# One third of the gate and up rows computed with the two matrices side by side, its last 21 rows without shared products

## The chip, the cores and the metric

The kernel runs on one core of a Trainium2 chip. The metric is the device time of one execution in microseconds. The core's engines run side by side and meet only at semaphores: TensorE (PE; its weight loads are listed apart as PEld), VectorE (DVE), ScalarE (ACT), GpSimd (POOL) and SyncE (SP, which issues most DMAs here).

## The reference, cut to what matters

A token has 1024 numbers, which are 8 components of 128. A small matrix per batch entry is applied first, then a feed-forward net whose linear maps are octonion products with ternary weights:

```python
y = einsum('bct,bcd->bdt', x, cond_weights[itok])            # (32, 64, 1024): 2048 tokens
gate = oct_ternary_linear(y, w_gate)                         # 8 components of 341 rows
up   = oct_ternary_linear(y, w_up)
h    = silu(gate) * up
out  = x + oct_ternary_linear(h, w_down)
# oct_ternary_linear: M = einsum('jik,jod->koid', S_OCT, Wq);  out = einsum('...id,koid->...ko', xp, M)
```

S_OCT holds a sign for every pair of components, so each output component k is a sum over the 8 input components i of a signed 341 x 128 matrix times y_i. Wq is -1, 0 or 1 times one scale for each of w_gate, w_up and w_down.

## The kernel before, in words

The 2048 tokens are cut into 8 tiles T of 256. Every operand of a large product is split into two float16 parts, "hi" and "lo", so each product is two matmuls (the loop over e). The 341 rows of a component are three windows w: 128, 128 and 85, the last padded with zeros to 128. A chunk c is one window of a pair of components (K, K+4), with both matrices m (0 gate, 1 up): 12 chunks a tile, c = 4w + K.

Sign relations between the components let the products be shared. A table (`gate_table`, `up_table`, built once in tile 0) holds sums and differences of weight blocks, and `y_op` holds the 8 components and 6 sums of them (14 operands). Of a chunk, PE makes (all through `group`, L1013 to L1018, whose every matmul is 128 x 128 weights times 256 tokens):

- `shared_pair` (even chunks only): 2 matrices x 2 terms x 2 parts = 8 matmuls into `bank_q`;
- `shared`: 8 matmuls into `bank_pr(s)`, s = c % 2;
- `own`: 2 matrices x 2 halves h x 4 terms x 2 parts = 32 matmuls into `bank_r(s, 0)` for gate and `bank_r(s, 1)` for up.

A bank is 512 float32 on 128 partitions. Chunks alternate between two sets of three banks. ACT (`chunk`, L640 to L654) copies the shared product out (`q_sb`, L646), applies SiLU to the gate bank in place (L652), and in `split_h` of the chunk before copies h to float16 (`h_op`, hi part, L613) and to float32 (`h_f`, L618). DVE (`chunk`, from L847) makes p = shared product +- q (L723), subtracts for the lo part of the h before (`h_lo`, L825), adds p to the gate bank and then to the up bank (L843, or two half-width L723 operations for K = 1), and multiplies SiLU(gate) by up (L870). These queues are in order. `own` of a chunk waits until `h_lo` and `h_f` of the chunk two before are done, since that frees the gate bank; `shared` waits for the p two before.

After the chunks comes `down`: for each window 64 products with `h_op` (`down_c`, 128 columns) and 32 with `z_op` (`down_u`, 256 columns) over both halves of the tile, 288 matmuls in all (L1108). `z_op` is made from `h_f` in six rounds k, two a window: POOL adds pairs and then the results (`round_of_z`, L531; k = 5 on DVE), ACT rounds to float16 (`z_hi`, L632), DVE makes the lo part (`z_lo`, L830). `Z_LO_AFTER` says after which chunk z_hi and z_lo of a round are queued: {6: 0, 7: 1, 10: 2, 11: 3}. POOL also turns the sums of the tile before back to outputs (`back`, L443).

The next tile's operands are made inside this one: `y_round(T + 1, r)` (L1003) after chunks 1, 2, 4 and 5 (`Y_AFTER`), each followed on ACT by `copy_y` (L588, L591), which the next `y_round` waits for since all use one bank; `row_norms` (L1010) after chunk 7; and on DVE `scales_of_tile` (L782 to L809) after chunk 8. Tile 7 has none of these. In tile 0, DVE also makes the ternary weights (`ternary`, L747 and L749) and the tables (`build_table`) of window 1 after chunks 0 and 2 and of window 2 after chunks 4 and 6, and PE and ACT mix the down weights (`mix`, L981, `mix_out`, L667) at chunks 6 to 11; ACT makes `down_c` (L705) after chunks 8 to 11.

SP's DMAs load x, the residual and the small matrices and store the outputs; their order is not touched.

## Time and profile before

| | |
|---|---|
| median of 3 runs | 723.91 us (722.75 to 724.21) |
| the profiled execution | 724.41 us, of which span 722.6 us |
| PE, PEld busy | 95%, 86% |
| DVE, ACT, POOL busy | 75%, 46%, 49% |
| granted TensorE clock, mean | 0.987 of full |

A share of busy time is a mean over the whole span. The chain of waits goes back from the last instruction to whatever released it, so an engine's share of that chain says how much of the time it alone set. In a timeline the start of an instruction and the start of the next one on the same engine lie less than one duration apart when the two overlap; "idle before" names the engine and line that ended a wait.

### The profile page before, as it was taken

What the parts mean: (1) busy time and instruction counts of PE and PEld (TensorE: products, weight loads), DVE (VectorE), ACT (ScalarE), POOL (GpSimd) and SP (SyncE); (2) the same over time, 40 slices, a digit from 0 to 9 for tenths busy, and PEclk for the clock granted to TensorE, in tenths of its full rate; (3) what the DMA queues carried; (4) which work ended last, traced back from release to release, by engine and by line L of the source; (5) the groups of instructions that cost most, each with busy time, mean ns of one, the idle gap of its engine ahead of it and who ended that gap; (6) DMA issues with size and microseconds to landing.
All of it is one profiled execution on the core that took longest, in us unless ns stands there. A gap on an engine that the chain in (4) does not pass through costs nothing.

```text
span 722.6 us, 17130 instructions
## 1 busy us (share of the span) xinstructions
PE 687.3 (95%) x7046; PEld 625.0 (86%) x7046; DVE 538.6 (75%) x867; ACT 332.3 (46%) x530; POOL 352.5 (49%) x409
## 2 busy tenths in 40 slices
PE   3679998999999999999999999999999999999995
PEld 3468887999999989999899999999899998988895
DVE  1898956767876688676877678766877678777877
ACT  5543485155444546255452555344452554434531
POOL 0200557435736466344856356364753357464553
PEclk9799999999999999999999999999999999999999
DMA  8100003021002110031001110031000300021001
GB/s 327 59 2 1 1 2 122 30 89 64 1 2 88 33 61 2 2 118 63 1 2 52 66 63 2 2 117 62 4 1 11 108 2 1 2 88 31 1 2 59
DMA packets 10576, 31.51 MB, mean 44 GB/s; under 512 B 3330, under 2 KB 3330, under 8 KB 10370
## 3 DMA queue, kind: packets, MB, share of 16 engines
q1 hardware_dynamic: 9906, 28.81, 11.2%
q10 hardware_dynamic: 592, 1.61, 0.7%
q8 instruction: 56, 0.92, 0.5%
q14 instruction: 22, 0.18, 0.1%
HBM read 22.02 MB, written 8.39 MB: 42 GB/s over the span
## 4 chain that ended last, share of the span: by engine, by line
PE 85%; DVE 7%; ACT 3%; issue 2%; POOL 1%; DMA 1%; ACTq 0%; DVEq 0%; POOLq 0%
PE ps L1016 58%; PE ps L1108 21%; PE ps L1003 4%; DMA cond_bd<-in_L_cond_weights_dram 1%; DVE pu_sb L723 1%; ACT down_c L705 1%; POOL z_f L531 1%; PE ps L1010 1%; DVE o_sb L443 1%; ACT z_op L632 1%; DVE ps L843 1%; POOL h_pairs L531 1%; DVE z_op L830 0%; ACT ps L652 0%; DVE gate_table L723 0%
## 5 line engine op out<-in xcount | busy, mean ns | idle before, releaser
L1016 PE MATMUL ps<-y_op,gate_table 128*128 128x256 f16 x2112 | 273.0, 275 | 5.7 <-DVE y_op L816 4.2
L1016 PE MATMUL ps<-y_op,up_table 128*128 128x256 f16 x2112 | 270.7, 273 | 0.2 <-DVE up_table L768 0.2
L1016 PEld LDWEIGHTS ps<-y_op,gate_table 128*128 128x128 f16 x2112 | 207.6, 99 | 30.6 <-DVE y_op L816 4.3
L1016 PEld LDWEIGHTS ps<-y_op,up_table 128*128 128x128 f16 x2112 | 207.1, 98 | 25.1 <-DVE up_table L768 0.7
L531 POOL TENSOR_TENSOR h_pairs<-h_f 128x256 f32<-128x256 f32 (+1 forms) x128 | 121.1, 975 | 151.8 <-ACT h_f L618 94.1
L531 POOL TENSOR_TENSOR z_f<-h_pairs 128x512 f32<-128x512 f32 x80 | 102.7, 1305 | 102.6 <-DVE z_op L830 100.8
L652 ACT ACTIVATE ps<-ps,small 128x512 f32<-128x512 f32 x96 | 63.6, 662 | 175.5 <-DVE ps L843 125.4
L443 POOL TENSOR_TENSOR o_sb<-o_sb,wd_sb 128x256 f32<-128x256 f32 (+1 forms) x150 | 88.3, 626 | 92.7 <-DVE wd_sb L891 91.5
L1108 PE MATMUL ps<-down_c,h_op 128*128 128x128 f16 x1536 | 93.1, 220 | 3.0 <-ACT down_c L705 3.0
L723 DVE TENSOR_TENSOR pu_sb<-ps,q_sb 128x512 f32<-128x512 f32 x96 | 65.8, 686 | 38.7 <-ACT q_sb L646 26.0
L1108 PEld LDWEIGHTS ps<-down_c,h_op 128*128 128x128 f16 x1536 | 89.8, 98 | 4.0 <-ACT down_c L705 3.1
L1108 PE MATMUL ps<-down_u,z_op 128*128 128x256 f16 x768 | 90.8, 274 | 1.5 <-DVE z_op L830 1.5
L830 DVE TENSOR_TENSOR z_op<-z_f,z_op 128x1024 f16<-128x1024 f32 x40 | 49.8, 1246 | 44.7 <-ACT z_op L632 44.7
L825 DVE TENSOR_TENSOR h_op<-ps,h_op 128x512 f16<-128x512 f32 x96 | 65.8, 685 | 23.0 <-ACT h_f L618 23.0
L1108 PEld LDWEIGHTS ps<-down_u,z_op 128*128 128x128 f16 x768 | 73.9, 98 | 9.8 <-DVE z_op L830 1.6
L870 DVE SCALAR_TENSOR_TENSOR ps<-pu_sb,small,ps 128x512 f32<-128x512 f32 x96 | 72.4, 755 | 11.5 <-ACT ps L652 1.6
L613 ACT ACTIVATE h_op<-ps 128x512 f16<-128x512 f32 x96 | 57.5, 599 | 35.3 <-DVE ps L870 33.7
L843 DVE TENSOR_TENSOR pu_sb<-ps,pu_sb 128x512 f32<-128x512 f32 x72 | 49.4, 686 | 31.2 <-PE ps L1016 31.0
L632 ACT ACTIVATE z_op<-z_f 128x1024 f16<-128x1024 f32 x40 | 42.1, 1053 | 36.9 <-POOL z_f L531 36.9
L618 ACT ACTIVATE h_f<-ps 128x512 f32<-128x512 f32 x96 | 57.7, 601 | 0.0
L843 DVE TENSOR_TENSOR ps<-ps,pu_sb 128x512 f32<-128x512 f32 x72 | 49.8, 691 | 4.2 <-PE ps L1016 3.2
L1003 PE MATMUL ps<-cond_bd,x_in 128*128 128x128 f32 x256 | 35.3, 285 | 13.3 <-DMA cond_bd<-in_L_cond_weights_dram 11.1
(75 smaller groups left out, 480.7 us busy)
## 6 DMA issues: line engine op xcount, KB each, us to landing
x_in<-in_x_dram SPq DMA_DIRECT2D x8, 1024.0 KB, 5.3
o_sb<-in_x_dram SPq DMA_DIRECT2D x16, 512.0 KB, 3.6
out_dram<-o_sb SPq DMA_DIRECT2D x15, 512.0 KB, 2.7
h_op<-in_L_ffn_w_gate_dram ACTq DMA_DIRECT2D x3, 512.0 KB, 6.8
h_op<-in_L_ffn_w_up_dram SPq DMA_DIRECT2D x3, 512.0 KB, 7.4
z_op<-in_L_ffn_w_down_dram SPq DMA_DIRECT2D x1, 1536.0 KB, 11.4
out_dram<-o_sb SPq DMA_DIRECT2D x2, 256.0 KB, 2.1
cond_bd<-in_L_cond_weights_dram SPq DMA_DIRECT2D x30, 16.0 KB, 3.0
```

What stands on the lines that cost most here:

```text
L443: last = eng.tensor_tensor(dst, dst, wd_sb[:, s, k1, r0, h, :], ALU.add if sign > 0 else ALU.subtract)
L531: return pool.tensor_tensor(dst, a, b, ALU.add if sign > 0 else ALU.subtract)
L613: act.activation(h_op[:, c, :, 0, :], bank_r(s, 0), ACT.Copy).then_inc(h_hi_ready, 1)
L618: act.activation(h_f[:, c], bank_r(s, 0), ACT.Copy).then_inc(h_copied, 1)
L652: act.activation(bank_r(s, 0), bank_r(s, 0), ACT.Silu, scale=gate_scale(T)).then_inc(silu_ready, 1)
L723: return dve.tensor_tensor(dst, a, b, ALU.add if sign > 0 else ALU.subtract)
L825: dve.tensor_tensor(h_op[:, c, :, 1, :], bank_r(s, 0), h_op[:, c, :, 0, :], ALU.subtract).then_inc(h_lo_ready, 1)
L843: return dve.tensor_tensor(dst, bank, pm.broadcast_to([P, 2, TOK]), ALU.add)
L870: dve.scalar_tensor_tensor(out=bank_r(s, 0), in0=u_sb[:], scalar=up_scale(T), in1=bank_r(s, 0), op0=ALU.mult, op1=ALU.mult).then_inc(h_rea ...
L1003: mm = pe.matmul(bank_y(T, r)[:, i, P * s:P * s + P], x_in[:, s, f:f + P], cond_bd[:, s, :], start=True, stop=True)
L1016: mm = pe.matmul(dst, table[m][:, slot, q, :], y_op[:, op, e, :], start=(i == 0 and e == 0), stop=(i == len(terms) - 1 and e == 1))
L1108: mm = pe.matmul(banks[bank][:, place], operand[:, P * s:P * s + P], weights, start=(bank not in begun), stop=(last and i == ends[bank]), ...
```

## The change

The three windows are reordered so that the partly filled one (85 rows) is second, in chunks 4 to 7. In it, gate and up stand side by side in one weight tile: 64 gate rows in columns 0 to 63, 64 up rows in columns 64 to 127 (`mid_table`), so one matmul serves both. `shared_pair` makes 4 matmuls instead of 8 (of one half K // 2 only), `shared` 4 instead of 8, `own` 16 instead of 32. Gate and up of a chunk are then the two halves of the partitions of one bank. ACT copies the up half to SBUF (`mid_u`), DVE's one addition of p serves both, and the multiplication for chunk c - 1 and `h_lo` of chunk c - 2 follow it. Chunks 4 to 7 have four banks (0, 3, 1, 4).

That covers 64 of the 85 rows. The other 21 (padded to 32) are made directly: two groups `rest(T, i)`, i = 0, 1, after chunk 7 (and after `row_norms`), each with 2 component pairs x 8 components x 2 parts = 32 matmuls, whose 128 columns are gate and up of both components of the pair, 32 rows each (`direct`, built by 16 more DVE operations in tile 0). Each group has two ACT operations before its multiplication (`rest_silu`), four after (`split_rest`) and two subtractions on DVE (`rest_lo`). `own` of chunks 8 and 9 waits for `rest_lo` and `rest_copied` of groups 0 and 1, whose banks they use. z_hi and z_lo of rounds 0 and 1 move from after chunks 6 and 7 to after chunks 7 and 8. POOL's rounds 2 and 3 wait for `rest_copied`. Operations on this window's h and z have 96 partitions. The y rounds stay after chunks 1, 2, 4 and 5 and the scales after chunk 8.

```diff
+    MID, HALF, REST = 1, P // 2, P // 4
+    assert NQ == 3 and count // (8 * P) - 2 * P <= HALF + REST
+    ROWS = [P, HALF + REST, P]
...
+    SCALES_AFTER = 8
...
-    Z_LO_AFTER = {6: 0, 7: 1, 10: 2, 11: 3}
+    Z_LO_AFTER = {7: 0, 8: 1, 10: 2, 11: 3}
...
-        table = [sb("gate_table", [P, NSLOT, NQ, P], F16), sb("up_table", [P, NSLOT, NQ, P], F16)]
+        table = [sb("gate_table", [P, NSLOT, NQ - 1, P], F16), sb("up_table", [P, NSLOT, NQ - 1, P], F16)]
+        mid_table = sb("mid_table", [P, NSLOT, 2, HALF], F16)
+        direct = sb("direct", [P, 3, 8, 2, 2, REST], F16)
...
+        def bank_mid(K):
+            return ps[:, (0, 3, 1, 4)[K], :].rearrange("p (h t) -> p h t", h=2)
+        def bank_mid_pr(K):
+            return ps[:, 3 * (K % 2) + 2, :].rearrange("p (i t) -> p i t", i=2)[:, K // 2]
+        def mid_u(i):
+            return ud_sb[:].rearrange("p s r h o -> p (s r h o)").rearrange("p (i a t) -> p i a t", i=2, a=2)[0:HALF, i % 2]
+        def bank_rest(i):
+            return ps[:, 3 * i, :].rearrange("p (k t) -> p k t", k=2)
...
             def round_of_z(T, k):
                 n = (NR - 1) * T + k
                 pool.wait_ge(h_copied, NC * T + 4 * (k // 2) + 4)
+                if k // 2 == MID:
+                    pool.wait_ge(rest_copied, 2 * T + 2)
...
+            def rest_silu(T, i):
+                n = 2 * T + i
+                act.wait_ge(rest_done, n + 1)
+                act.wait_ge(h_ready, NC * T + 4 * MID + 3 + i)
+                act.activation(mid_u(i), bank_rest(i)[HALF:P], ACT.Copy)
+                gate = bank_rest(i)[0:HALF]
+                act.activation(gate, gate, ACT.Silu, scale=gate_scale(T)[0:HALF]).then_inc(rest_silu_ready, 1)
+            def split_rest(T, i):
+                act.wait_ge(rest_h_ready, 2 * T + i + 1)
+                slots_of_i = slice(4 * MID + 2 * i, 4 * MID + 2 * i + 2)
+                for h in range(2):
+                    last = act.activation(h_op[HALF:HALF + REST, slots_of_i, h, 0, :],
+                                          bank_rest(i)[REST * h:REST * h + REST], ACT.Copy)
+                last.then_inc(rest_hi_ready, 1)
+                for h in range(2):
+                    last = act.activation(h_f[HALF:HALF + REST, slots_of_i, h, :],
+                                          bank_rest(i)[REST * h:REST * h + REST], ACT.Copy)
+                last.then_inc(rest_copied, 1)
...
+                    if w == MID:
+                        act.activation(q_sb[:, K // 2], bank_q[:, K // 2], ACT.Copy).then_inc(q_copied, 1)
+                    else:
+                        act.activation(q_sb[:], bank_q, ACT.Copy).then_inc(q_copied, 1)
+                if c == 4 * (MID + 1):
+                    split_rest(T, 1)
+                elif c > 0 and (w != MID or K == 0):
                     split_h(T, c - 1)
                 if T == 0:
...
                 act.wait_ge(g_ready, n + 1)
-                act.activation(bank_r(s, 0), bank_r(s, 0), ACT.Silu, scale=gate_scale(T)).then_inc(silu_ready, 1)
+                if w == MID:
+                    if T > 0 and K == 0:
+                        act.wait_ge(wd_ready, SUB * T)
+                    act.wait_ge(h_ready, n - 1)
+                    act.activation(mid_u(K), bank_mid(K)[HALF:P], ACT.Copy).then_inc(u_ready, 1)
+                    gate = bank_mid(K)[0:HALF]
+                    act.activation(gate, gate, ACT.Silu, scale=gate_scale(T)[0:HALF]).then_inc(silu_ready, 1)
+                    if K > 0:
+                        split_h(T, c - 1)
+                else:
+                    act.activation(bank_r(s, 0), bank_r(s, 0), ACT.Silu, scale=gate_scale(T)).then_inc(silu_ready, 1)
...
+                    if c == 4 * MID + 3:
+                        split_h(T, c)
+                        rest_silu(T, 0)
+                        split_rest(T, 0)
+                        rest_silu(T, 1)
...
-                    return table[m][:, a:a + n, w, :]
+                    return mid_table[:, a:a + n, m, :] if w == MID else table[m][:, a:a + n, w // 2, :]
...
+                if w == MID:
+                    for h in range(2):
+                        for high in range(2):
+                            src = t[:, 4 * (h ^ high):4 * (h ^ high) + 4, HALF:HALF + REST]
+                            signs = [kind[h] for kind in KINDS[high]]
+                            for sign in (1, -1):
+                                kinds = [k for k in range(3) if signs[k] == sign]
+                                step = kinds[-1] - kinds[0] or 1
+                                dst = direct[:, kinds[0]:kinds[-1] + 1:step, 4 * high:4 * high + 4, m, h, :]
+                                dve.tensor_scalar(dst, src.rearrange("p (a j) o -> p a j o", a=1).broadcast_to(
+                                    [P, len(kinds), 4, REST]), float(sign), None, ALU.mult).then_inc(direct_built, 1)
...
+            def rest_h(T, i):
+                dve.wait_ge(rest_silu_ready, 2 * T + i + 1)
+                gate = bank_rest(i)[0:HALF]
+                dve.scalar_tensor_tensor(out=gate, in0=mid_u(i), scalar=up_scale(T)[0:HALF], in1=gate,
+                                         op0=ALU.mult, op1=ALU.mult).then_inc(rest_h_ready, 1)
+            def rest_lo(T, i):
+                dve.wait_ge(rest_copied, 2 * T + i + 1)
+                slots_of_i = slice(4 * MID + 2 * i, 4 * MID + 2 * i + 2)
+                for h in range(2):
+                    last = dve.tensor_tensor(h_op[HALF:HALF + REST, slots_of_i, h, 1, :],
+                                             bank_rest(i)[REST * h:REST * h + REST],
+                                             h_op[HALF:HALF + REST, slots_of_i, h, 0, :], ALU.subtract)
+                last.then_inc(rest_lo_ready, 1)
...
+            def mid_h(T, c):
+                n, K = NC * T + c, CHUNKS[c][0]
+                dve.wait_ge(silu_ready, n + 1)
+                dve.wait_ge(u_ready, n + 1)
+                gate = bank_mid(K)[0:HALF]
+                dve.scalar_tensor_tensor(out=gate, in0=mid_u(K), scalar=up_scale(T)[0:HALF], in1=gate,
+                                         op0=ALU.mult, op1=ALU.mult).then_inc(h_ready, 1)
+            def mid_chunk(T, c):
+                n, u = NC * T + c, NU * T + c // 2
+                K, bank = CHUNKS[c][0], bank_mid(CHUNKS[c][0])
+                dve.wait_ge(q_copied, u + 1)
+                dve.wait_ge(pr_done, n + 1)
+                if K == 0:
+                    dve.wait_ge(u_ready, n)
+                else:
+                    dve.wait_ge(g_ready, n)
+                p = p_sb[:, 0]
+                signed_add(p, bank_mid_pr(K), q_sb[:, K // 2], G2[K // 2] if K % 2 else 1).then_inc(p_ready, 1)
+                if K == 0:
+                    h_lo(T, c - 1)
+                dve.wait_ge(p_ready, n + 1)
+                dve.wait_ge(gate_done, n + 1)
+                dve.wait_ge(up_done, n + 1)
+                add_p(bank, bank, 0, K).then_inc(g_ready, 1)
+                if K > 0:
+                    mid_h(T, c - 1)
+                if K > 1:
+                    h_lo(T, c - 2)
...
+                if c == 4 * (MID + 1):
+                    dve.wait_ge(g_ready, n)
...
+                if c == 4 * (MID + 1):
+                    rest_lo(T, 1)
+                elif c > 0:
...
+                    if c == 4 * MID + 3:
+                        mid_h(T, c)
+                        h_lo(T, c - 1)
+                        h_lo(T, c)
+                        rest_h(T, 0)
+                        rest_lo(T, 0)
+                        rest_h(T, 1)
...
+            def group(dst, m, q, terms):
+                for i, (slot, op) in enumerate(terms):
...
+                for m in [K // 2] if q == MID else range(2):
+                    mm = group(bank_q[:, m], m, q, [(slots[wq[K // 2, b]], 12 + b) for b in range(2)])
...
+                terms = [(slots[wpr[K, b][0]], 8 + wpr[K, b][1]) for b in range(2)]
+                if q == MID:
+                    mm = group(bank_mid_pr(K), None, q, terms)
+                else:
+                    for m in range(2):
+                        mm = group(bank_pr(s)[:, m], m, q, terms)
                 mm.then_inc(pr_done, 1)
...
+            def mid_own(T, c):
+                n, K = NC * T + c, CHUNKS[c][0]
+                if K < 2:
+                    pe.wait_ge(h_lo_ready, n - 1)
+                    pe.wait_ge(h_copied, n - 1)
+                else:
+                    pe.wait_ge(u_ready, n - 3)
+                for h in range(2):
+                    mm = group(bank_mid(K)[:, h], None, MID, [(slots[wr[h, K, p][0]], wr[h, K, p][1]) for p in range(4)])
+                    mm.then_inc(up_done if h else gate_done, 1)
...
+            def rest(T, i):
+                pe.wait_ge(h_lo_ready, NC * T + 4 * MID + i + 1)
+                pe.wait_ge(h_copied, NC * T + 4 * MID + i + 1)
+                if T == 0:
+                    pe.wait_ge(direct_built, 16)
+                for k in range(2):
+                    for j in range(8):
+                        for e in range(2):
+                            mm = pe.matmul(bank_rest(i)[:, k], direct_weights(2 * i + k, j), y_op[:, j, e, :],
+                                           start=(j == 0 and e == 0), stop=(j == 7 and e == 1))
+                mm.then_inc(rest_done, 1)
...
+                if q == MID:
+                    mid_own(T, c)
+                    return
+                if 0 <= c - 4 * (MID + 1) < 2:
+                    pe.wait_ge(rest_lo_ready, 2 * T + c - 4 * (MID + 1) + 1)
+                    pe.wait_ge(rest_copied, 2 * T + c - 4 * (MID + 1) + 1)
...
-                                yield (f"c{h}", corr[h, v, p][0], h_op[:, 4 * w + p, v, e], down_c[:, w, v, p, h])
+                                yield (f"c{h}", corr[h, v, p][0], h_op[0:ROWS[w], 4 * w + p, v, e],
+                                       down_c[0:ROWS[w], w, v, p, h])
...
+                pe.wait_ge(rest_lo_ready, 2 * (T + 1))
...
+                    if c == 4 * MID + 3:
+                        for i in range(2):
+                            rest(T, i)
...
-        return a.reshape(*a.shape[:axis], -1, P, *a.shape[axis + 1:])
+        return a.reshape(*a.shape[:axis], -1, P, *a.shape[axis + 1:]).take([0, 2, 1], axis)
...
```

## Rows read from the trace of the kernel before

**Rows 1.** The page: busy us, share of the span, instructions of each engine.

```profile
PE 687.3 (95%) x7046; PEld 625.0 (86%) x7046; DVE 538.6 (75%) x867; ACT 332.3 (46%) x530; POOL 352.5 (49%) x409
```

**Rows 2.** Chain of waits in tile 3: start us, us, engine, line, count.

```profile
302.15 9.61 PE ps L1016 x88
311.76 0.89 PE ps L1003 x8
...
329.29 4.37 PE ps L1016 x40
...
344.15 0.87 PE ps L1010 x8
345.03 19.21 PE ps L1016 x176
364.24 21.20 PE ps L1108 x288
```

**Rows 3.** Timeline of DVE, tile 4, chunks 0 and 1.

```profile
391.50 0.70 DVE L843 TENSOR_TENSOR ps<-ps,pu_sb 128x512 f32<-128x512 f32 x1
392.11 0.68 DVE L843 TENSOR_TENSOR pu_sb<-ps,pu_sb 128x512 f32<-128x512 f32 x1
392.98 0.76 DVE L870 SCALAR_TENSOR_TENSOR ps<-pu_sb,small,ps 128x512 f32<-128x512 f32 x1 [0.20 <-ACT ps L652]
393.65 0.68 DVE L723 TENSOR_TENSOR pu_sb<-ps,q_sb 128x512 f32<-128x512 f32 x1
394.96 0.69 DVE L825 TENSOR_TENSOR h_op<-ps,h_op 128x512 f16<-128x512 f32 x1 [0.63 <-ACT h_f L618]
395.57 0.75 DVE L723 TENSOR_TENSOR ps<-ps,pu_sb 128x256 f32<-128x256 f32 x2
396.23 0.74 DVE L723 TENSOR_TENSOR pu_sb<-ps,pu_sb 128x256 f32<-128x256 f32 x2
```

**Rows 4.** Timeline of ACT: tile 3 at chunks 4 and 5, tile 4 at chunk 0.

```profile
335.56 0.60 ACT L646 ACTIVATE q_sb<-ps 128x512 f32<-128x512 f32 x1
336.03 0.62 ACT L613 ACTIVATE h_op<-ps 128x512 f16<-128x512 f32 x1
...
338.88 0.66 ACT L652 ACTIVATE ps<-ps,small 128x512 f32<-128x512 f32 x1 [1.74 <-DVE ps L843]
339.47 1.05 ACT L632 ACTIVATE z_op<-z_f 128x1024 f16<-128x1024 f32 x1
...
392.23 0.66 ACT L652 ACTIVATE ps<-ps,small 128x512 f32<-128x512 f32 x1 [1.79 <-DVE ps L843]
393.77 0.60 ACT L613 ACTIVATE h_op<-ps 128x512 f16<-128x512 f32 x1 [0.88 <-DVE ps L870]
394.27 0.59 ACT L618 ACTIVATE h_f<-ps 128x512 f32<-128x512 f32 x1
```

**Rows 5.** Timeline of DVE, tile 3: z_lo, the first scale operation, what follows, y_lo.

```profile
341.28 1.22 DVE L830 TENSOR_TENSOR z_op<-z_f,z_op 128x1024 f16<-128x1024 f32 x1
...
351.76 0.41 DVE L782 TENSOR_REDUCE small<-ps 128x1 f32<-128x256 f32 x1
...
353.71 0.68 DVE L723 TENSOR_TENSOR pu_sb<-ps,q_sb 128x512 f32<-128x512 f32 x1
...
377.97 4.21 DVE L816 SCALAR_TENSOR_TENSOR y_op<-y_f,small,y_op 128x1024 f16<-128x1024 f32 x3
```

**Rows 6.** Busy us by stretch, tile 0: PE, PEld, DVE, ACT, POOL, clock, DMA.

```profile
60.00:70.00 10.00, 10.00 (x95) 8.97 (x93) 8.88 (x28) 2.20 (x4) 0.00 (x0) 1.00 0.01 2
70.00:80.00 10.00, 9.40 (x110) 8.49 (x109) 9.69 (x21) 5.50 (x10) 1.25 (x2) 1.00 0.01 2
80.00:90.00 10.00, 9.88 (x115) 8.93 (x114) 9.68 (x13) 4.14 (x8) 9.28 (x7) 1.00 0.00 1
```

**Rows 7.** Timeline of DVE, tile 0: the gate table of window 1.

```profile
37.98 1.16 DVE L723 TENSOR_TENSOR gate_table<-z_op 128x512 f16<-128x512 f16 x4
39.05 0.22 DVE L764 TENSOR_SCALAR gate_table<-z_op 128x256 f16<-128x256 f16 x1
```

More of the change, by code:

```diff
@@ L612, in split_h @@
                     act.wait_ge(tern_ready[1], c // 4 + 1)
-                act.activation(h_op[:, c, :, 0, :], bank_r(s, 0), ACT.Copy).then_inc(h_hi_ready, 1)
+                mid = CHUNKS[c][1] == MID
+                rows = slice(0, HALF) if mid else slice(0, P)
+                bank = (bank_mid(CHUNKS[c][0]) if mid else bank_r(s, 0))[rows]
+                act.activation(h_op[rows, c, :, 0, :], bank, ACT.Copy).then_inc(h_hi_ready, 1)
                 if T > 0 and c % 4 == 0:
@@ L935, in _ @@
                         z_lo(T, z_after[c])
[L936 removed]
+                    if T > 0 and T + 1 < NT and c == SCALES_AFTER:
                         scales_of_tile(T + 1)
@@ L1011, in row_norms @@
                 mm.then_inc(norm_done, 1)
-            def group(dst, m, terms):
-                for i, (slot, q, op) in enumerate(terms):
+            def group(dst, m, q, terms):
+                for i, (slot, op) in enumerate(terms):
+                    weights = mid_table[:, slot] .rearrange("p m o -> p (m o)") if q == MID else table[m][:, slot, q // 2, :]
                     for e in range(2):
-                        mm = pe.matmul(dst, table[m][:, slot, q, :], y_op[:, op, e, :],
+                        mm = pe.matmul(dst, weights, y_op[:, op, e, :],
                                        start=(i == 0 and e == 0), stop=(i == len(terms) - 1 and e == 1))
```

72 lines of the change are left out of this document (45 added, 27 removed).

## The prediction

> **What bounds the kernel now.** I read the page first: PE is busy 95% of the span, DVE 75%, ACT 46% and POOL 49% [rows 1]. Then the chain in order of time. In tile 3 it is PE alone, piece after piece with no gap: 88 matmuls in 9.61 us, so 0.1092 us a matmul of 256 columns, 0.89 us for a y round, 0.87 for the row norms, 21.20 for the 288 products of down. 528 x 0.1092 + 4 x 0.89 + 0.87 + 21.20 = 83.29 us a tile, which is the distance from 302.15 to 385.44 [rows 2]. Six tiles (1 to 6) are like this; tile 7 differs by what it leaves out, and tile 0 is bound by DVE, which is busy 28.3 of 30 us in its middle [rows 6]. Last the timelines, for how far DVE and ACT lag behind PE. The lag is what this change puts at risk: they have slack now only because a chunk takes PE 44 matmuls, 4.80 us, and DVE about 3.1 us.
>
> Three measures are needed. DVE issues a 512-wide addition every 0.60 us (391.50 to 392.11), a pair of 256-wide ones every 0.66, so 0.33 each, and a multiplication every 0.67 [rows 3]. ACT issues a copy every 0.48 and a SiLU every 0.59 [rows 4]. A result passes from DVE to ACT in 0.03 us (392.11 + 0.09 = 392.20 to 392.23) and from ACT to DVE in 0.10 (394.27 + 0.59 = 394.86 to 394.96) [rows 3, 4]; to and from PE I take 0.05, between these two.
>
> **PE's part.** Window 1 had 4 chunks x 44 = 176 matmuls. It gets 24 + 20 + 24 + 20 = 88, plus 2 x 32 direct ones: 152. 24 x 0.1092 = 2.62 us less per tile. The operations on 96 partitions in down keep their 128 or 256 columns and I count them unchanged. No row has a 96-row product; the bounds are nothing gained, and at worst a 128-column product at the price of a 256-column one, 64 x (0.109 - 0.055) = 3.5 us more a tile. The Trainium skill (TensorE: Matmul & The Clock Gate, LDWEIGHTS) states that a weight load costs by its columns and not by its rows; by that nothing changes.
>
> **DVE's and ACT's part.** A chunk of window 1 costs DVE 0.33 (p) + 0.60 + 0.67 + 0.60 = 2.2 us, or 2.3 with its wait for its own p, instead of 3.1. ACT gets a half q every other chunk, the copy of up, SiLU and two copies of h: 0.12 + 0.48 + 0.59 + 0.96 = 2.15 us, and each y round's two copies 0.96 more. PE's chunk falls to 2.4 us. So in chunks 4 to 7 three engines have one pace, where PE had nearly twice the others' time. Then each rest group gives ACT 6 operations (2.99 us) and DVE 3 (0.67 + 1.20 = 1.87), for 3.49 us of PE. No row has an operation on 64 or 32 partitions. I price them by their free size, as the nearest rows; the lower bound is by partitions, half for 64, a quarter for 32. The Trainium skill (TensorEngine Tiling (Array Packing), PSUM Bottleneck) speaks against the change in the same way: packing makes PE faster but not the emptying of PSUM, which can become the limit.
>
> I laid these durations end to end by each engine's queue order and waits, t = 0 at the tile's first product (302.15 in tile 3). Chunk 4 begins at 21.0 (329.29 less 48 matmuls and a y round) [rows 2].
>
> - Chunk 4's products end at 23.62, but DVE first makes h_lo(3), which waits for ACT's h_f(3) to 23.84. Adding p runs 24.44 to 25.13, ACT's copy of up and SiLU to 26.3, the two copies of y round 2 to 27.32. Y round 3 may start at 27.37; PE is there at 26.69. Wait: 0.68.
> - ACT then has SiLU(5), split 4, the copies of y round 3 (29.58 to 30.54) and only then q for chunk 6. DVE idles 2.9 us before p(6) at 31.0. Adding p(7) is done at 34.5 while PE left chunk 7 at 33.06. ACT: up and SiLU of 7, splits of 6 and 7 to 37.54, rest_silu(0) to 38.7; DVE multiplies to 39.53; ACT's four copies to 41.62; DVE's two subtractions 41.72 to 43.01. Own of chunk 8 starts at 43.06. PE (norms, 64 direct, 16 shared matmuls) is there at 42.67. Wait: 0.39, then 0.05 at own of 9.
> - ACT goes on with rest_silu(1), z_hi(0), q(8) and split_rest(1) to 46.04. DVE: rest_lo(1) from 46.14, two additions, multiply at 48.84, then z_lo(1) at 49.85 (a move of this change: 1.2 us [rows 5]), then the scales, 1.95 us [rows 5], p(9) at 52.94, h_lo(8) to 54.23. Own of chunk 10 waits for h_lo(8): 54.28, PE is there at 52.73. Wait: 1.55.
> - DVE stays behind through chunks 9 and 10: h_lo(10) ends at 63.2, and down waits for it from 62.14. Wait: 1.12.
>
> Sum 3.79 against 2.62 saved: **+1.17 us a tile, +7.0 for six.** With ACT to DVE at 0.05 it would be +0.80 a tile. What stays hidden: y_lo of the next tile ended at 382.18 (377.97 + 4.21 [rows 5]), 3.3 us before the tile's end [rows 2], which is more than DVE falls behind PE; z rounds 2 and 3 begin on POOL, half idle [rows 1], when rest_copied(1) comes, at 46, and down wants them after 62. If that cover failed, the 3.3 us would be used up first.
>
> **Tile 7** has no norms, y rounds or scales, so PE arrives earlier and the rest chain starts earlier. The same laying out gives waits of 0.52 (own 5 for h_lo(3)), 1.02 (rest 0 for h_lo(4)), 0.86 and 0.05 (own 8, 9 for rest_lo) and 0.72 (down): 3.17, less 2.62, and 0.1 at the end: +0.65.
>
> **Tile 0.** PE's saving is worth nothing there. DVE's work falls by 4 x (3.07 - 2.19) = 3.5 and grows by 3.7 for the rest groups. Each half-width table costs some 0.5 less, and each direct table 8 operations, between the 0.14 a 256-wide operation takes before the next starts (39.05 to 39.19 [rows 7]) and its 0.22, some 1.2: +0.7 twice, one of which falls into waits. So +0.9 of work. New waits of DVE: 0.5 for its own p, and for ACT in the rest chain 0.7 + 0.4 + 2.3 + 1.7 = 5.1, since with chunk 8's four more copies there is nothing else to do. The 1.75 us that DVE idled before [rows 6] go into these. 0.9 + 5.6 - 1.75 = **+4.7** (1 to 7).
>
> Sum: 7.0 + 0.65 + 4.7 = +12.3 on the profiled execution's 724.41, and that lies 0.5 above the median of 723.91: **736 us.**
>
> **The rivals.**
> 1. PE keeps its bound (faster). If operations on 64 and 32 partitions cost by partitions, every wait above but the y round's goes, and 7 x 2.6 less 0.7 x 6 to nothing is left: 14 to 18 us, tile 0 about even: 706 to 710. Not slower than before it is from under 1.7 us of waits a tile, for then 6 x (2.62 - 1.7) pays for tiles 0 and 7. For it: PE in tile 3 has never been without work [rows 2], and buffers grow from two sets to four banks. Against: nothing in the trace shows a duration that falls with partitions. Chance 0.15.
> 2. Half the waits. DVE and ACT catch up in the y rounds better than I lay out: 1.9 us a tile of waits instead of 3.8 gives -0.7 x 6, tile 7 -1, tile 0 +3: -2, 722. The waits hang on chains of ten hand-offs, each of them uncertain by some 0.05. Chance 0.17.
> 3. Slower still, by the products in down on 96 partitions: at the upper bound 3.5 x 8 = 28 us, 764. For it: such products stand nowhere in the trace. Against: a row count changes none of the durations seen. Chance 0.03.
> 4. The lag is worse than laid out: 1 us more of waits a tile, as each hand-off to and from PE at 0.10 would begin to give, 743. Chance 0.07.
> That the change does not do what it says I see no room for: the counts of products follow from the code.
>
> **How the numbers follow.** Forecast 0.58, its own range 730 to 741 (+0.5 to +1.5 a tile, tile 0 +2 to +6). A measurement of this kernel tells no change from one of 0.2%, 1.4 us. Faster is all of rival 1 and over half of 2, 0.26; same 0.06; slower 0.68. The range reaches from 713, between rivals 1 and 2, to 743.
>
> **What would show it.** PE's matmuls at L1016 and in rest fall by 192, to 4032. In a middle tile PE, which had no idle time, must show four waits: before a y round on ACT's y_sq, before own of chunk 8 on rest_lo (DVE), before own of 10 and before down on h_lo (DVE), the third the longest. The distance between the starts of two middle tiles must be 84.0 to 84.8; under 82 proves the laying out wrong, and a copy on 64 partitions near 0.3 us would say why. Tile 0 should be 3 to 6 us longer. A down of over 21.5 us speaks for rival 3.

## The result, and the profile after

The changed kernel takes 751.95 us (median, 750.72 to 753.5), the kernel before 723.98 us: ratio 1.0396, interval 1.0381 to 1.0412. So it is slower, as forecast, but by 28 us and not by 12, and 752 lies outside the range of 713 to 743. The profiled execution took 750.72 us, its span is 748.9 against 722.6: +26.3 us to be explained.

The page of the changed kernel: busy us, share of the span, instructions; then three groups by line, operation and tile (busy us, mean ns | idle before). They answer to [rows 1].

```profile
PE 672.6 (90%) x6854; PEld 603.4 (81%) x6854; DVE 540.7 (72%) x891; ACT 400.6 (53%) x658; POOL 353.9 (47%) x409
...
L1185 PE MATMUL ps<-y_op,gate_table 128*128 128x256 f16 x1408 | 182.9, 276 | 30.4 <-DVE h_op L944 13.5
...
L1185 PE MATMUL ps<-y_op,mid_table 128*128 128x256 f16 x704 | 81.0, 273 | 0.5 <-DVE h_op L930 0.5
...
L1240 PE MATMUL ps<-y_op,direct 128*128 128x256 f16 x512 | 57.2, 273 | 1.1 <-DVE h_op L930 1.1
```

TensorE's busy time fell by 14.7 us and its instructions by 192, as counted, and the span still grew: its share went from 95% to 90%. ACT has 128 operations and 68 us more. The idle time stands before the full chunks' own products (the gate_table group): 30.4 us, of which 13.5 are put down to L944, VectorE's subtractions for the rest groups (`rest_lo`); L930 is the same for the chunks (`h_lo`).

The timeline of TensorE in tile 4 shows where (start us, us, instructions; in brackets the idle time before and what ended it). The first line is the tile's first product.

```profile
312.93 1.91 PE L1185 MATMUL ps<-y_op,gate_table 128*128 128x256 f16 x16
...
333.93 2.78 PE L1185 MATMUL ps<-y_op,mid_table 128*128 128x256 f16 x24
336.55 1.06 PE L1170 MATMUL ps<-cond_bd,x_in 128*128 128x128 f32 x8
337.44 2.35 PE L1185 MATMUL ps<-y_op,mid_table 128*128 128x256 f16 x20
340.55 1.16 PE L1170 MATMUL ps<-cond_bd,x_in 128*128 128x128 f32 x8 [0.76 <-ACT y_sq L634]
...
356.92 1.92 PE L1185 MATMUL ps<-y_op,gate_table 128*128 128x256 f16 x16 [0.80 <-DVE h_op L944]
...
362.07 1.92 PE L1185 MATMUL ps<-y_op,gate_table 128*128 128x256 f16 x16 [0.61 <-DVE h_op L944]
...
369.29 1.92 PE L1185 MATMUL ps<-y_op,gate_table 128*128 128x256 f16 x16 [1.80 <-DVE h_op L930]
...
378.15 1.95 PE L1318 MATMUL ps<-down_c,h_op 128*128 128x128 f16 x32 [0.83 <-issue]
```

Where [rows 2] had no gap there are five, at the five places that were laid out: y round 3, own products of chunks 8, 9 and 10, down. The wait before down is printed as "issue", but VectorE's `h_lo` of chunk 10, for which it waits, ended at 378.05, 0.10 us before it. The printed waits run from modelled ends; by 0.1092 us a matmul the fourth is 369.29 - (366.88 + 4 x 0.1092) = 1.97, and the five are 0.93, 0.96, 0.77, 1.97 and 0.99, together 5.62 us. Down starts at 291.72 in tile 3 and at 378.15 in tile 4, 86.43 us apart; 83.29 - 2.62 = 80.67 of products leave 5.76 us, of which these five are 5.62. The 26.3 us are then: down of tile 0 starts at 117.20 and not at 112.56, +4.64; from there to down of tile 6 it takes 520.25 us and not 501.38, +18.87, which is +3.14 for each of six distances; what follows, tile 7 and the end, is +2.79.

### The profile page after: what moved, and what is told of

The parts are those of the page before. It is cut to its first block and busy times, and to the rows that moved or that the text cites. A ratio compares the mean times of both kernels' runs of the same rounds, so it can differ in the third digit from the quotient of the medians.

```text
span 748.9 us, 16944 instructions
## 1 busy us (share of the span) xinstructions
PE 672.6 (90%) x6854; PEld 603.4 (81%) x6854; DVE 540.7 (72%) x891; ACT 400.6 (53%) x658; POOL 353.9 (47%) x409
## 5 line engine op out<-in xcount | busy, mean ns | idle before, releaser
L1185 PE MATMUL ps<-y_op,gate_table 128*128 128x256 f16 x1408 | 182.9, 276 | 30.4 <-DVE h_op L944 13.5
L571 POOL TENSOR_TENSOR h_pairs<-h_f 128x256 f32<-128x256 f32 (+3 forms) x128 | 124.2, 996 | 140.8 <-ACT h_f L664 89.4
L1185 PE MATMUL ps<-y_op,up_table 128*128 128x256 f16 x1408 | 179.9, 273 | 0.4 <-DVE up_table L859 0.4
L1185 PEld LDWEIGHTS ps<-y_op,gate_table 128*128 128x128 f16 x1408 | 136.9, 99 | 53.2 <-DVE h_op L944 17.6
L571 POOL TENSOR_TENSOR z_f<-h_pairs 128x512 f32<-128x512 f32 (+1 forms) x80 | 101.2, 1285 | 138.6 <-DVE z_op L951 136.9
L1318 PE MATMUL ps<-down_c,h_op 128*128 128x128 f16 (+1 forms) x1536 | 92.8, 220 | 8.5 <-issue 5.5
L1318 PEld LDWEIGHTS ps<-down_c,h_op 128*128 128x128 f16 (+1 forms) x1536 | 89.1, 98 | 11.1 <-issue 7.3
L1318 PE MATMUL ps<-down_u,z_op 128*128 128x256 f16 (+1 forms) x768 | 91.2, 275 | 1.9 <-DVE z_op L951 1.9
L930 DVE TENSOR_TENSOR h_op<-ps,h_op 128x512 f16<-128x512 f32 (+1 forms) x96 | 65.6, 684 | 27.0 <-ACT h_f L664 26.9
L1318 PEld LDWEIGHTS ps<-down_u,z_op 128*128 128x128 f16 (+1 forms) x768 | 74.0, 99 | 10.5 <-DVE z_op L951 2.1
L1185 PE MATMUL ps<-y_op,mid_table 128*128 128x256 f16 x704 | 81.0, 273 | 0.5 <-DVE h_op L930 0.5
```

The lines of the kernel that those rows point to most:

```text
L571: return pool.tensor_tensor(dst, a, b, ALU.add if sign > 0 else ALU.subtract)
L930: dve.tensor_tensor(h_op[rows, c, :, 1, :], bank, h_op[rows, c, :, 0, :], ALU.subtract).then_inc(h_lo_ready, 1)
L1185: mm = pe.matmul(dst, weights, y_op[:, op, e, :], start=(i == 0 and e == 0), stop=(i == len(terms) - 1 and e == 1))
L1318: mm = pe.matmul(banks[bank][:, place], operand[:, P * s:P * s + P], weights, start=(bank not in begun), stop=(last and i == ends[bank]), ...
```

## The experiments

"Tile" below is the distance of two starts of down in the middle of each kernel's own trace: before 83.29, changed 86.43. The kernel before took 724.09, 722.58 and 723.05 us beside the three groups of runs.

Three kernels were run once only (rest groups not evacuated, no rest groups, scales moved); the others 4 to 8 times.

**The order of the thirds alone**, the kernel before with only this:

```diff
-        return a.reshape(*a.shape[:axis], -1, P, *a.shape[axis + 1:])
+        return a.reshape(*a.shape[:axis], -1, P, *a.shape[axis + 1:]).take([0, 2, 1], axis)
```

> The kernel before with only the order of its thirds changed: the partly filled one second, in the layout of the weights as they are read in, and the products, roundings and sums as before, on 128 rows. All theories: no operation changes its size or its place, only the addresses of the loads; the whole stays at 722 to 726 us. If the order alone cost something, the first tile's loads would be later, and the whole 726 or more.

724.03 us, ratio 1.0005 (0.9992 to 1.0017). The order costs nothing; what costs is how the third is made.

**No evacuation of the rest groups.**

```diff
-                        rest_silu(T, 0)
-                        split_rest(T, 0)
-                        rest_silu(T, 1)
...
-                    split_rest(T, 1)
...
-                        rest_h(T, 0)
-                        rest_lo(T, 0)
-                        rest_h(T, 1)
...
-                    rest_lo(T, 1)
```

> Left out of the changed kernel: everything that empties the rest groups (SiLU, multiplication, copies, subtractions; 12 ACT and 6 DVE operations a tile), so the 21 rows do not enter the output; the 64 direct products a tile stay. Theory A: the chain loses 7.3 us of ACT and 4.3 of DVE; PE's waits before chunks 8, 9 and 10 go, those before a y round (0.8) and before down (1.0) stay: a middle tile of 82.5 to 82.9, tile 0 about 3.6 shorter, the whole about 723 to 726, that is only as fast as before the change. Rival C (the side-by-side window itself is too fast for ACT and DVE, whatever the rest): waits of 2 us or more stay before chunks 8 to 10 and the whole stays above 735.

720.8 us; tile 82.68. The h of the 21 rows is set to zero once, and TensorE's and GpSimd's waits for these operations are left out with them. In the middle tiles it is theory A: the waits before chunks 8, 9 and 10 are gone, y round 3 (0.76 printed) and down (0.79) stay. The whole is 2 us below its range, and tile 0 became 2.5 us shorter (114.73), not 3.6. So 3.75 of the 5.76 us of waits a tile hang on 12 small ScalarE and 6 VectorE operations. TensorE's saving is real, but about three quarters of it would still be given back by the other two waits: 83.29 - 82.68 = 0.6 us of 2.62 is left.

**No rest groups at all**, their 64 products taken away too.

```diff
-                        for i in range(2):
-                            rest(T, i)
```

> Leaves out the direct products of the 21 last rows of the partly filled third and all that ScalarE and VectorE do on them (the rows are set to zero once by GpSimd); these 21 rows are therefore missing from the result. Beside the run that left out the evacuation alone (middle tile 82.68 us, whole 720.8) it takes 32 products of 128 by 256 a tile from TensorE, 32 x 0.1092 = 3.49 us. If TensorE alone sets the pace there (theory), a middle tile takes 79.2 us, or down to 78.5 as the two waits left shift, and the whole 8 x 3.5 = 28 us less than that run: 690 to 697. Rival: with the 3.5 us gone, ScalarE and VectorE are late for the third's shared groups, and new waits of about 1 us a tile appear: whole 700 to 705.

699.4 us, tile 79.46. The expectation miscounts: two groups of 32 are 64 products, 6.99 us, so TensorE alone would need 80.67 - 6.99 = 73.7. Measured against that the theory falls, and what the rival says of new waits holds, though 699.4 is just under its range: of 6.99 us taken from TensorE only 3.22 were gained, the rest became waits in new places.

```profile
243.62 1.16 PE L1161 MATMUL ps<-cond_bd,x_in 128*128 128x128 f32 x8 [0.76 <-ACT y_sq L635]
253.92 1.92 PE L1176 MATMUL ps<-y_op,gate_table 128*128 128x256 f16 x16 [1.71 <-DVE h_op L926]
264.54 1.92 PE L1176 MATMUL ps<-y_op,gate_table 128*128 128x256 f16 x16 [0.84 <-DVE h_op L926]
274.24 1.96 PE L1305 MATMUL ps<-down_c,h_op 128*128 128x128 f16 x32 [1.67 <-DVE h_op L926]
```

These are a middle tile's waits in that kernel: before y round 3, chunk 8, chunk 10 and down. With the shared groups alone ScalarE and VectorE already are behind TensorE.

**The scales moved** into VectorE's gap of 2.45 us before rest_lo(0):

```diff
                         rest_h(T, 0)
+                        if T > 0 and T + 1 < NT:
+                            scales_of_tile(T + 1)
                         rest_lo(T, 0)
...
-                    if T > 0 and T + 1 < NT and c == SCALES_AFTER:
-                        scales_of_tile(T + 1)
```

> Changed from the changed kernel: DVE's ten scale operations (1.95 us) move from after chunk 8 to the gap of 2.45 us in which DVE waits for the rest group's copies, ahead of rest_lo(0). Theory A: from chunk 4 to chunk 10 ACT and DVE are one chain and set the pace, so what leaves DVE's queue on that chain comes back in full: PE's wait before own of chunk 10 (1.80 us) goes, a middle tile falls from 86.4 to 84.5, the whole by 6 x 1.95 = 11.7 us to 740. Theory B: each PE wait has its own cause, mainly the banks that rest_lo must free before chunks 8 and 9: the wait before chunk 10 shrinks but reappears before down, and the whole falls by under 3 us, 749 to 752.

747.27 us, tile 85.31: between the two theories. The wait before chunk 10 is gone, as laid out, but that before down rose from 0.83 to 1.65. A z_lo in chunk 10 had become long, partly beside a pair addition of GpSimd (VectorE, then GpSimd, same kernel):

```profile
374.76 2.04 DVE L951 TENSOR_TENSOR z_op<-z_f,z_op 96x1024 f16<-96x1024 f32 x1 [0.21 <-ACT z_op L699]
```

```profile
373.23 2.50 POOL L571 TENSOR_TENSOR h_pairs<-h_f 96x512 f32<-96x512 f32 x2 [0.17 <-POOL z_f L571]
```

It takes 1.22 us elsewhere [rows 5]. Six tiles gained 6 x 1.12 = 6.7 us, the span only 3.4 (745.5 for 748.9), since tile 0's down started at 120.85 instead of 117.20. The edit does not reach tile 0: that is mostly the clock of this execution (last section).

**The rest groups in other banks**, so that chunks 8 and 9 can start their own products at once:

```diff
-            return ps[:, 3 * i, :].rearrange("p (k t) -> p k t", k=2)
+            return ps[:, 3 * i + 2, :].rearrange("p (k t) -> p k t", k=2)
...
+                late = 0 <= c - 4 * (MID + 1) < 2
+                (own if late else shared)(T, c)
```

> Changed from the changed kernel: the two rest groups use the banks of the shared products, and in chunks 8 and 9 PE makes the own products before the shared ones, so that own no longer waits for rest_lo. Theory A (chain of ACT and DVE): PE's waits of 0.80 and 0.61 us before chunks 8 and 9 go, and the wait before own of chunk 10 grows from 1.8 to about 3.5; the tile stays at 86.4 and the whole at 752 within 2 us. Theory B (banks): both waits go and nothing takes their place: 1.7 us a tile, 12 in all, 740.

756.8 us (ratio 1.0463, 1.0442 to 1.0483), tile 87.11. The waits before 8 and 9 are gone and the one before 10 went from 1.80 to 3.58. The banks were not the limit; the chain on ScalarE and VectorE is, and TensorE only meets it one chunk later. The whole is 3 us above theory A's range: behind that wait the products ran at half speed in most tiles (last section). The one middle tile in which they did not took 86.44, as theory A has it; the others took 86.89 to 88.06.

**The order of the copies alone**: 16-bit and 32-bit copy of one half, then of the other, where both 16-bit ones came first.

```diff
                 for h in range(2):
-                    last = act.activation(h_op[HALF:HALF + REST, slots_of_i, h, 0, :],
+                    act.activation(h_op[HALF:HALF + REST, slots_of_i, h, 0, :],
                                    bank_rest(i)[REST * h:REST * h + REST], ACT.Copy)
-                last.then_inc(rest_hi_ready, 1)
-                for h in range(2):
                     last = act.activation(h_f[HALF:HALF + REST, slots_of_i, h, :],
```

> Changed from the changed kernel: the order of ACT's four copies of a rest group, so that two copies from the same 32 partitions follow each other. In the changed kernel each of the four starts 0.60 us after the one before, where copies of the earlier kernel start every 0.48. Theory P: a copy that starts on other partitions does not overlap the one before; then two of the three gaps fall to 0.48, a tile by 0.2 to 0.5, the whole by 2 to 4 us. Theory Q: operations on 32 partitions never overlap; then the gaps stay 0.60 and the time does not change.

752.75 us (1.0394, 1.0374 to 1.0414), tile 86.19. ScalarE in the changed kernel, then in this one:

```profile
347.74 0.59 ACT L730 ACTIVATE ud_sb<-ps 64x512 f32<-64x512 f32 x1
348.36 0.65 ACT L732 ACTIVATE ps<-ps,small 64x512 f32<-64x512 f32 x1
...
350.38 0.59 ACT L664 ACTIVATE h_f<-ps 64x512 f32<-64x512 f32 x1
350.99 0.59 ACT L671 ACTIVATE ud_sb<-ps 64x512 f32<-64x512 f32 x1
351.60 0.65 ACT L673 ACTIVATE ps<-ps,small 64x512 f32<-64x512 f32 x1
353.06 1.18 ACT L679 ACTIVATE h_op<-ps 32x512 f16<-32x512 f32 x2 [0.81 <-DVE ps L936]
354.26 1.18 ACT L683 ACTIVATE h_f<-ps 32x512 f32<-32x512 f32 x2
355.47 0.59 ACT L671 ACTIVATE ud_sb<-ps 64x512 f32<-64x512 f32 x1
356.08 0.65 ACT L673 ACTIVATE ps<-ps,small 64x512 f32<-64x512 f32 x1
356.66 1.04 ACT L699 ACTIVATE z_op<-z_f 128x1024 f16<-128x1024 f32 x1
357.61 0.58 ACT L717 ACTIVATE q_sb<-ps 128x512 f32<-128x512 f32 x1
358.21 1.18 ACT L679 ACTIVATE h_op<-ps 32x512 f16<-32x512 f32 x2
359.42 1.18 ACT L683 ACTIVATE h_f<-ps 32x512 f32<-32x512 f32 x2
```

```profile
355.40 0.59 ACT L679 ACTIVATE h_op<-ps 32x512 f16<-32x512 f32 x1 [0.81 <-DVE ps L934]
355.90 0.57 ACT L681 ACTIVATE h_f<-ps 32x512 f32<-32x512 f32 x1
356.48 0.59 ACT L679 ACTIVATE h_op<-ps 32x512 f16<-32x512 f32 x1
356.97 0.57 ACT L681 ACTIVATE h_f<-ps 32x512 f32<-32x512 f32 x1
357.57 0.59 ACT L671 ACTIVATE ud_sb<-ps 64x512 f32<-64x512 f32 x1
```

A copy lasts 0.57 to 0.59 us in both. In the first every copy of a rest group begins 0.60 after the last, and each reads other partitions than the one before; in the second the pairs on one half begin 0.50 and 0.49 apart, and only the change of half takes 0.58 and 0.60. That is theory P. The waits before 8 and 9 fell by 0.24 each (0.80 to 0.56, 0.61 to 0.37) and the one before 10 rose by 0.25 (2.05), as VectorE's z_lo ahead of it took 1.77 us instead of 1.52; so the tile won 0.24 us. The whole did not fall by the 2 to 4 us expected: in the profiled execution down of tile 0 started at 119.31, at a lower clock, and one middle tile took 86.88.

**Copies and subtractions by halves**: the order above, and VectorE subtracts the first half while ScalarE copies the second.

```diff
-                dve.wait_ge(rest_copied, 2 * T + i + 1)
                 slots_of_i = slice(4 * MID + 2 * i, 4 * MID + 2 * i + 2)
                 for h in range(2):
+                    dve.wait_ge(rest_copied, 4 * T + 2 * i + h + 1)
```

> ScalarE copies a rest group by halves (16-bit and 32-bit copy of one half, then of the other), and VectorE subtracts the first half's rounded values while ScalarE copies the second half, on other partitions. Beside the run that changed the order of the copies alone (middle tile 86.19 us, whole 752.8), one of the two subtractions of 0.69 us leaves the chain ahead of chunk 8. Theory (the serial chain of ScalarE's copies and VectorE's subtractions sets the waits before chunks 8 and 9): those two waits together lose 0.7 to 1.2 us; some of it comes back in the wait before chunk 10, where VectorE's scales of the next tile stand; a middle tile takes 85.2 to 85.9 us and the whole 745 to 751. Rival: all of it comes back before chunk 10, a middle tile stays at 86.1 to 86.3 and the whole at 751 to 754.

744.16 us (1.0293, 1.0257 to 1.033), tile 85.40. In the tile the theory holds: the wait before 8 is no longer printed, that before 9 is 0.38, and 0.13 came back before 10 (1.93), where z_lo took 1.66 us. The whole is 1 us better than its range, with down of tile 0 at 118.79. To let the subtractions start ahead of the 32-bit copies of the same half was not tried: by the Trainium skill (PSUM — Partial Sum Buffer, PSUM bank collisions raise a hardware error) two engines may not read one bank on the same 32 partitions at a time; no run here shows it.

**The y rounds before the third:**

```diff
-    Y_AFTER = {1: 0, 2: 1, 4: 2, 5: 3}
+    Y_AFTER = {0: 0, 1: 1, 2: 2, 3: 3}
```

> The four rounds of the next tile's y stand after chunks 0, 1, 2, 3 and no longer after 1, 2, 4, 5, so that none lies inside the partly filled third's shared chunks. Theory: the waits come from the chain of the rest groups behind chunk 7 (copy, SiLU, product, four copies, two subtractions), which the y rounds do not touch, so a middle tile stays at 86.4 us (85.9 to 86.6) and the whole at 750 to 754. Rival: the y rounds' copies and sums inside the third make ScalarE and VectorE late for its chunks and so for the rest groups; then the waits before chunks 8 and 9 fall by about half, 0.9 to 1.5 us a tile, and the whole is 741 to 746.

754.44 us (1.0435, 1.0413 to 1.0458), tile 86.72. The wait of y round 3 (0.76) is gone, small ones stand in the third (0.18) and before the rest groups (0.28), and the one before chunk 8 grew from 0.80 to 1.31. The rival falls. The theory is right that the time does not go down, and both numbers lie just above its ranges: the move made a tile 0.29 us longer.

**z's roundings put back** to where they were:

```diff
-    Z_LO_AFTER = {7: 0, 8: 1, 10: 2, 11: 3}
+    Z_LO_AFTER = {6: 0, 7: 1, 10: 2, 11: 3}
```

> z's roundings of rounds 0 and 1 stand after chunks 6 and 7 again, as in the kernel before, and no longer after 7 and 8. If VectorE is the engine that is late in the gap between chunk 7 and chunk 10 (theory), the round 1 roundings, which wait for GpSimd's sums, now stand in that gap and ahead of the rest groups' last subtraction: a middle tile goes from 86.4 to 87.5 to 88.5 us, and the whole to 760 to 770. Rival: the order of these roundings does not matter, since the rest groups' chain on ScalarE is what ends last; the whole stays within 1.5 us of 752.

763.63 us (1.0558, 1.0538 to 1.0579), tile 87.93: the theory. The wait before chunk 8 is 2.50 and a new one of 1.39 stands before the rest groups; the one before chunk 10 is gone. Without that part of the change it would be 12 us slower still.

**The best order I found**: the scales in the gap, the y rounds after chunks 1 to 4, and

```diff
                         rest_silu(T, 0)
+                        if T > 0:
+                            z_hi(T, 0)
                         split_rest(T, 0)
```

> The changed kernel in the best order that I find by laying out ScalarE's and VectorE's operations by their measured durations: the next tile's scales in the gap ahead of rest_lo(0), the y rounds after chunks 1 to 4, and z's high part of round 0 ahead of the rest group's copies. Theory (the rest groups add more to the chain of ScalarE and VectorE than any order can hide, and TensorE's 2.6 us a tile go there): a middle tile takes 83.5 to 84.5 us, against 83.3 before and 86.4 in the changed kernel, and the whole 732 to 742, still slower than before. Rival: the loss is one of order alone; then all but the wait before the down products goes, a middle tile takes 81.6 to 82.7, and the whole is 712 to 722, faster than before. A third possibility by the runs so far: what is won in the middle tiles comes back in the first tile as a lower granted clock, 2 to 3 us, within the upper part of the theory's range.

738.26 us (1.0218, 1.0197 to 1.0239), tile 84.05, the theory. **With the halves beside it:**

> The best order so far (middle tile 84.05 us, whole 738.3) with the copies and subtractions by halves. Its wait before chunk 8 is 1.50 us, and the same 0.7 us of the second subtraction and 0.2 us of the copies leave it. Theory: the middle tile takes 83.2 to 83.7 us and the whole 731 to 736, still slower than before, since the second group's copies are then late for chunk 9. Rival: the second group is late by as much already, the middle tile stays at 83.9 to 84.2 and the whole at 736 to 739. Faster than before (under 722) would take a middle tile under 82.5 us, with the first tile's 4 us more to be made good.

733.18 us (1.0149, 1.0131 to 1.0166), tile 83.65. This theory holds too. TensorE's waits in a middle tile of the last kernel:

```profile
338.81 7.16 PE L1239 MATMUL ps<-y_op,direct 128*128 128x256 f16 x64 [0.28 <-DVE h_op L929]
...
348.56 1.92 PE L1184 MATMUL ps<-y_op,gate_table 128*128 128x256 f16 x16 [0.84 <-DVE h_op L943]
...
367.54 1.95 PE L1317 MATMUL ps<-down_c,h_op 128*128 128x128 f16 x32 [1.10 <-issue]
```

With all the order that I could find, a middle tile is still 0.36 us longer than before the change (83.65 against 83.29), and tile 0 costs 4 us more (116.57). No version here that makes the whole output beats the kernel before; the two that were faster leave out work on the 21 rows.

## Why the prediction was right and wrong

**Right:** the sign and its reason; TensorE's part; the places of all five waits, and that the one before chunk 10 is the longest.

**Right in the number, in part by luck:** tile 0, +4.7 forecast, and down there is 4.64 later. The two profiled executions differ in clock: in the same chunk of tile 0 the 32 own products and the y round before them took 6.15 us in the kernel before (50.65 to 56.80) and 4.49 in the changed one (50.71 to 55.20). At the same clock the difference would be about 6.3 us, an estimate from these. The term's parts are not shown either: without the evacuation, in an execution with the same fall of the clock as before, 2.2 us stay (114.73).

Rival 3 is refuted by TensorE's rows in the changed kernel, where 96 rows cost as much as 128, and by down, which takes 21.21 us (291.72 to 312.93):

```profile
L1318 PE MATMUL ps<-down_c,h_op 128*128 128x128 f16 x1024 | 62.1, 220 | 8.5 <-issue 5.5 <-ACT down_c L789 3.0
L1318 PE MATMUL ps<-down_c,h_op 96*128 96x128 f16 x512 | 31.4, 219 | 0.0
L1318 PE MATMUL ps<-down_u,z_op 128*128 128x256 f16 x512 | 60.9, 276 | 1.9 <-DVE z_op L951 1.9
L1318 PE MATMUL ps<-down_u,z_op 96*128 96x256 f16 x256 | 30.6, 273 | 0.0
```

The condition of rival 1 is refuted by ScalarE's rows above: copies on 64 and 32 partitions take 0.57 to 0.59 us, as those on 128 did [rows 4]. Rival 2 went the wrong way: the lag was worse, not better, than laid out. Rival 4 (743) had the right direction at half the size, for another reason: it wanted hand-offs to TensorE of 0.10 us, and the one behind the first rest group takes 0.06 (VectorE's subtractions end at 355.48 + 1.38 = 356.86, the products start at 356.92).

**The step that failed** is the laying out of a middle tile, "Sum 3.79 against 2.62 saved: +1.17 us a tile". The mechanism was right, the size was not: 5.76 us, so +3.14. The price that it had wrong is ScalarE's: a copy every 0.48 us, where the rest groups and the copies of up need 0.60 to 0.63 where they change partitions. Six tiles are 11.8 of the 14.0 us that the forecast lacked (6 x (3.14 - 1.17)); tile 7, laid out the same way as +0.65, came to +2.79 and is the rest. Against the forecast the single waits were 0.93 for 0.68, 0.96 for 0.39, 0.77 for 0.05, 1.97 for 1.55 and 0.99 for 1.12.

What was in their place can be followed with t counted from 312.93, the tile's first product. Up to chunk 5 the plan nearly holds: chunk 4 at 21.00 (21.0), VectorE's addition at 337.51, 24.58 (24.44). Then ScalarE's start-to-start times depart from it. I had priced a copy of up at 0.48 until the next start [rows 4], but the operations around it are on other partitions, and such a change takes 0.60 to 0.63.

- Two of these changes lie in chunks 4 and 5 (338.23 to 338.86, 340.72 to 341.34). VectorE's sum of chunk 6 starts at 344.25, t = 31.32, planned 31.0.
- Three more lie between chunk 7's copy of up and SiLU of the first rest group (347.74 to 348.36; 350.38, 350.99, 351.60 above). It ends at 39.32, planned 38.7.
- Three stand between the four copies: from the end of VectorE's product to theirs it took 2.41 us (353.03 to 355.44), planned 2.09. Own products of chunk 8 start at t = 43.99, planned 43.06.
- From there to the end of the second group's copies (360.60) it took 5.16 us, planned 4.42, with six more changes at 0.12 each.

VectorE shows the same:

```profile
352.28 0.75 DVE L936 SCALAR_TENSOR_TENSOR ps<-ud_sb,small,ps 64x512 f32<-64x512 f32 x1 [0.53 <-ACT ps L673]
355.48 1.38 DVE L944 TENSOR_TENSOR h_op<-ps,h_op 32x512 f16<-32x512 f32 x2 [2.45 <-ACT h_f L683]
356.89 0.75 DVE L936 SCALAR_TENSOR_TENSOR ps<-ud_sb,small,ps 64x512 f32<-64x512 f32 x1
...
360.63 1.38 DVE L944 TENSOR_TENSOR h_op<-ps,h_op 32x512 f16<-32x512 f32 x2 [1.07 <-ACT h_f L683]
...
364.56 1.52 DVE L951 TENSOR_TENSOR z_op<-z_f,z_op 128x1024 f16<-128x1024 f32 x1 [0.23 <-ACT z_op L699]
```

Two subtractions take 1.38 us, 0.69 each, where additions on unchanged partitions start 0.60 apart [rows 3].

At own of chunk 10 the tile is 2.08 us behind the plan (56.36 for 54.28). Of these 0.93 were there at chunk 8, the second group added about 0.7, and the rest came behind it, where z_lo(1) takes 1.52 us for 1.22. The run with the copies reordered shows the changes of partitions as a cause: it takes away some of them and nothing else, the starts move from 0.60 to 0.50 apart, and the waits before chunks 8 and 9 fall. The halves shorten the same chain and the tile falls by 1.03 us, but they also take a subtraction out of it. The changes around the copies of up were seen and not tested by themselves. Nor was the length of z_lo, though in both of these runs the wait before chunk 10 grew as z_lo did (by 0.25 and 0.13 us, z_lo by 0.25 and 0.14).

The chances had room for this in 4 alone, at 0.07. A price that is a little low at every step of a chain adds up and does not average out: the rival's 1 us a tile should have been a bound on one side of the forecast, and the range should have gone beyond 750.

## What to carry to other kernels

When a change takes products away, look at how many operations evacuate them: here the third's products fell by 14% (176 to 152 a tile) and ScalarE's and VectorE's operations in the whole kernel grew by 128 and 24, with the same 0.6 to 0.7 us each on 32, 64 or 128 partitions. An engine that had half its time free over the tile can still be late in the stretch that was changed, so lay out that stretch alone, with start-to-start times taken from pairs that are like the new ones (same partitions or not), and carry an error of one sign through the whole chain. A saving on TensorE is worth what is left after the next engine's lag: from 6.99 us less a tile, 3.22 were gained. Compare the first tile's clock in both profiles before you compare the wholes.

## What the runs showed of the hardware

**Overlap of successive operations is lost when the next one starts on other partitions.** ScalarE: 0.47 to 0.50 us from start to start on the same partitions, 0.58 to 0.63 on others, at a duration of 0.57 to 0.59. VectorE: 0.60 and 0.69 at a duration of 0.69. By these rows what counts is where the range starts, of what is read or of what is written: from 64 partitions to all 128, both from the first, ScalarE kept 0.48 (342.40 to 342.88 in the changed kernel), and from 128 to a copy that writes 32 in the upper half it took 0.60 (357.61 to 358.21). The Trainium skill (ScalarE: Activation LUTs, What ACT_TABLE_LOAD costs) says that activations back to back overlap by about 93 ns; the trace agrees, with 0.59 - 0.48 = 0.11 us, where the partitions stay.

**VectorE's 1024-wide subtraction from SBUF is longer beside GpSimd, but not each time.** 1.22 or 1.23 us with GpSimd idle, 1.52 in the changed kernel beside its y sum, 2.04 with the scales moved, partly beside its pair addition; in the best-order kernel it took 1.22 beside the same y sum. The Trainium skill (GPSIMD Engine Reference, Specifications) states that GpSimd shares its interfaces to SBUF with VectorE and meets contention from VectorE's instructions with two inputs there; the trace agrees in part.

**The first tile's clock falls behind waits, but not alike in every execution.** The stretch 50 to 60 us of the kernel before and of the changed kernel (PE, PEld, DVE, ACT and POOL busy, granted clock, DMA share, GB/s):

```profile
50.00:60.00 10.00, 9.35 (x70) 7.93 (x71) 6.83 (x16) 5.42 (x12) 0.00 (x0) 0.83 0.01 2
```

```profile
50.00:60.00 10.00, 9.29 (x84) 8.52 (x85) 8.87 (x27) 5.72 (x12) 0.00 (x0) 1.00 0.01 2
```

Up to 55 us both run the same products here, behind the same wait of 2.22 us for `y_sq`. The 16 own products behind the y round took 3.39 us in the kernel before and 1.91 in the changed kernel: 0.83 is a stretch partly at 1.2 and partly at 2.4 GHz. The stretch 90 to 100 us of the kernel before, the changed kernel, the one with the scales moved and the one without the evacuation:

```profile
90.00:100.00 10.00, 10.00 (x117) 9.12 (x115) 5.16 (x10) 8.30 (x17) 5.28 (x6) 1.00 0.01 2
```

```profile
90.00:100.00 10.00, 10.00 (x109) 8.85 (x107) 6.03 (x9) 7.30 (x14) 1.15 (x1) 0.95 0.01 2
```

```profile
90.00:100.00 10.00, 9.58 (x77) 7.42 (x78) 5.32 (x8) 6.43 (x13) 0.00 (x0) 0.68 0.00 0
```

```profile
90.00:100.00 10.00, 10.00 (x120) 9.15 (x119) 5.95 (x10) 7.13 (x14) 3.48 (x4) 1.00 0.01 2
```

At 0.68, 77 matmuls are done instead of 109. Before the fall stands the tile's first wait for the rest groups, 3.13 us both in the changed kernel (to 88.37; the 16 products after it took 3.21 us instead of 1.92) and with the scales moved (to 90.42; 3.59 us). The kernel before and the one without the evacuation have no such wait and stay at 1.00 in this stretch.

How long the clock stays low is not a matter of the kernel alone. In the runs with the scales moved, the y rounds moved, z's roundings put back and the best order, tile 0 is the same program as in the changed kernel, as these edits reach only later tiles. Down of tile 0 started at 120.85, 118.86, 120.95 and 118.58 there, and at 117.20 in the changed kernel. So one program's first tile differs by up to 3.75 us between executions, and neither the 4.64 us of tile 0 above nor a difference of 2 or 3 us between two wholes can be put down to an edit without looking at it.

In the kernel with other banks the wait of 3.58 us was followed by half-speed products in the middle tiles too: the 16 own products after it took 3.30, 2.33, 3.37, 1.92, 3.30 and 3.60 us in tiles 1 to 6. What decides whether the clock falls behind a wait, and for how long, stays open.
